# Turning the gathered token rows of a mixture-of-experts feed-forward with VectorE block transposes instead of TensorE transposes

## The reference, cut to what matters

```
gate = xs @ w_gate[e]              # 1024 -> 512
up   = xs @ w_up[e]                # 1024 -> 512
down = (silu(gate) * up) @ w_down[e]   # 512 -> 1024
```

## Time and profile before

| quantity | value |
|---|---|
| median of the three executions | 15,433.22 us |
| span of the profiled execution, first to last instruction | 15,412.0 us |
| time of the median that lies outside that span | 21.2 us |
| PE busy | 14,528.9 us (94%) |
| DVE, ACT, POOL busy | 41%, 21%, 25% |
| mean granted TensorE clock | 0.968 |
| DMA engines' busy share in routed tiles, in shared tiles | about 0.23, 0.62 |

### The profile page before, as it was taken

How to read it: one execution, slowest core, us unless ns; L and a number is a source line. 1 busy time by engine, 2 the same in 40 slices (tenths; PEclk the granted TensorE clock), 3 DMA queues, 4 the chain that set the end, 5 groups by cost and what they waited for, 6 DMA issues and landing times.

```text
span 15412.0 us, 212654 instructions
## 1 busy us (share of the span) xinstructions
PE 14528.9 (94%) x73632; PEld 12344.4 (80%) x73633; DVE 6313.4 (41%) x7679; ACT 3173.3 (21%) x4006; POOL 3896.2 (25%) x3973
## 2 busy tenths in 40 slices
PE   7878877749999999999999999999999999999999
PEld 7777777738888888888888888788888888888888
DVE  8998989941221222212221222322212111444554
ACT  3333333311111112211211222312111111111111
POOL 3344445541111111111111111111111111333333
PEclk9888888869999999999999999999999999999999
DMA  2233332241221222212221222322212111666666
GB/s 69 69 63 66 66 64 63 53 72 60 74 75 59 74 76 105 91 60 73 91 74 58 91 89 91 129 93 102 73 60 75 58 60 42 210 206 204 208 204 204
DMA packets 481191, 1445.61 MB, mean 94 GB/s; under 512 B 94385, under 2 KB 94385, under 8 KB 480834
## 3 DMA queue, kind: packets, MB, share of 16 engines
q0 software_dynamic: 286720, 890.00, 17.3%
q1 hardware_dynamic: 172738, 485.33, 11.5%
q10 hardware_dynamic: 21504, 67.13, 1.1%
HBM read 1037.89 MB, written 421.08 MB: 95 GB/s over the span
## 4 chain that ended last, share of the span: by engine, by line
PE 77%; DVE 0%; DMA 0%; issue 0%; ACT 0%; DVEq 0%; ACTq 0%; SPq 0%; POOLq 0%; POOL 0%
PE gps L1318 24%; PE ups L1318 24%; PE yps L1318 24%; PE xps L1325 4%; PE hps L1358 2%; DVE wlo L1246 0%; DMA raw<-in_L_ffn_w_up_dram 0%; ACT whi L1181 0%; DMA xg<-xnd,idx 0%; DVE yrow L1272 0%; DMA picked<-yd,gidx 0%; ACTq L1063 0%; DVEq L1063 0%; DVE xlo L1246 0%; DVE hlo L1246 0%
## 5 line engine op out<-in xcount | busy, mean ns | idle before, releaser
L1282 DVE TENSOR_TENSOR hb<-hb,ups 128x512 f32<-128x512 f32 x672 | 462.1, 688 | 6196.1 <-ACT hb L1200 6196.1
L1160 POOL DMA_INDIRECT yd<-yrow,yidx x544 | 575.6, 1058 | 7816.9 <-DVE yrow L1296 7816.9
L1318 PE MATMUL gps<-whi,xhi 128*128 128x512 f32 x5376 | 2157.4, 401 | 32.8 <-DVE wlo L1246 29.1
L1318 PE MATMUL ups<-whi,xlo 128*128 128x512 f32 x5376 | 2112.9, 393 | 0.0
L1318 PE MATMUL gps<-wlo,xhi 128*128 128x512 f32 x5376 | 2111.6, 393 | 0.0
L1318 PE MATMUL ups<-whi,xhi 128*128 128x512 f32 x5376 | 2111.3, 393 | 0.0
L1318 PE MATMUL gps<-whi,xlo 128*128 128x512 f32 x5376 | 2110.9, 393 | 0.0
L1318 PE MATMUL ups<-wlo,xhi 128*128 128x512 f32 x5376 | 2094.3, 390 | 0.0
L750 PE MATMUL yps<-khi,thi 128*128 128x288 f32 x4608 | 1481.8, 322 | 337.7 <-ACT ysb L436 193.8
L1200 ACT ACTIVATE hb<-gps 128x512 f32<-128x512 f32 x672 | 402.4, 599 | 6729.3 <-PE ups L1318 6719.1
L1318 PE MATMUL yps<-whi,hhi 128*128 128x512 f32 x5376 | 1725.9, 402 | 4.5 <-DVE hlo L1246 4.5
(11 more groups left out here) (161 smaller groups left out, 20294.0 us busy)
## 6 DMA issues: line engine op xcount, KB each, us to landing
raw<-in_L_ffn_w_gate_dram SPq DMA_DIRECT2D x128, 512.0 KB, 6.0
raw<-in_L_ffn_w_up_dram SPq DMA_DIRECT2D x128, 512.0 KB, 7.6
raw<-in_L_ffn_w_down_dram SPq DMA_DIRECT2D x64, 1024.0 KB, 6.9
cin<-in_ctx_dram SPq DMA_DIRECT2D x64, 512.0 KB, 5.0
xin<-in_x_dram SPq DMA_DIRECT2D x64, 512.0 KB
traw<-kpad SPq DMA_DIRECT2D x64, 512.0 KB, 4.2
xres<-in_x_dram SPq DMA_DIRECT2D x256, 128.0 KB, 2.6
x2d<-xres SPq DMA_DIRECT2D x64, 512.0 KB
```

The costliest lines, as they stand in the source:

```text
L1160: pool.indirect_dma_start(out=yd, in_=yrow[i][:, :], in_offset=None, out_offset=bass.IndirectOffsetOnAxis(ap=yidx[i][:, 0:1], axis=0), bou ...
L1282: dve.tensor_tensor(hb[:, :], hb[:, :], ups[:, :], ALU.mult).then_inc(h_done, 1)
L1318: ins = pe.matmul(ps, rows, w[:, chunk, i * 512:(i + 1) * 512], start=first and n == 0, stop=last_one and n == 2)
```

## The change

The eight PE transposes of the token rows go, with the PSUM tensor `xps`. The gather brings a quarter row per descriptor: four indirect DMAs per tile, where partition 32a+s receives, in slot q, quarter a of the tile's token 4s+q. For this the list is loaded as 32 rows of four numbers and written to four groups of partitions, and POOL adds the quarter's number (`xidx`). One DVE transpose instruction over 128x1024 float32, made of 32x32 blocks (`x_turn`), writes `xt` in SBUF, laid out with token rows along the free dimension. The rows of the gate and up weights are stored in the matching order, outside the kernel, with gate and up side by side, so that one DMA of 1 MB loads two chunks of both; the down weights are stored so that a partition's piece is contiguous. `x_high` and `x_low` read `xt` instead of PSUM.

The orders change too. ACT makes `x_high`(t+1) ahead of silu(t), DVE `x_low`(t+1) ahead of the multiplication, and `x_turn`(t+2) stands in DVE's order behind the split of the gate and up weights and ahead of the sums. POOL makes `load_list` and `gather` ahead of `fetch_picks`. Two of the four `picked` buffers go: pick k uses buffer k % 2, so that picks 2 and 3 can be fetched only when picks 0 and 1 of the same tile have been added. The gated rows keep their PE transposes.

```diff
@@ load_weights(sp, raw, w_ld, gate_up, down, before_unit)
-        for src, c in ((gate, 0), (up, I)):
-            sp.dma_start(raw[:, 2 * q:2 * q + 2, c:c + I],
-                         src[2 * q * P:(2 * q + 2) * P, :].rearrange("(k p) i -> p k i", p=P))\
-                .then_inc(w_ld[q], 16)
+        sp.dma_start(raw[:, 2 * q:2 * q + 2, :], gate_up[:, 2 * q:2 * q + 2, :]).then_inc(w_ld[q], 16)
@@ feed_forward
-        xg = [sb(f"xg{i}", [P, L]) for i in range(2)]
+        xg = [sb(f"xg{i}", [P, QUADS, L // QUADS]) for i in range(2)]
+        xt = sb("xt", [P, KX, P])
-        picked = [sb(f"picked{k}", [P, L]) for k in range(K // 2)]
+        picked = [sb(f"picked{k}", [P, L]) for k in range(2)]
-        xps = es.enter_context(nc.psum_tensor("xps", [P, 1024], F32))
@@ gpsimd
-                pool.dma_start(idx[slot][:, :], lists[bass.ds(row * P, P), :]).then_inc(idx_ld[slot], 16)
+                src = lists[bass.ds(row * P, P), :].rearrange("(o s q) n -> o s (q n)", o=1, q=QUADS)
+                pool.dma_start(idx[slot][:, :], src.to_broadcast([QUADS, SQ, QUADS])).then_inc(idx_ld[slot], 16)
...
-                wait(pool, xT_mm, t - 1 if not isinstance(t, int) else max(t - 1, 0))
+                wait(pool, x_turned, t - 1 if not isinstance(t, int) else max(t - 1, 0))
                 pool.wait_ge(idx_ld[slot], 16 * (turns + 1))
-                settle(pool, pool_turns)
-                pool.indirect_dma_start(out=xg[slot][:, :], out_offset=None, in_=xnd,
-                                        in_offset=bass.IndirectOffsetOnAxis(ap=idx[slot][:, 0:1], axis=0))\
-                    .then_inc(x_ld[slot], 16)
+                pool.tensor_tensor(xidx[slot][:, :], idx[slot][:, :], quad[:, :], ALU.add).then_inc(xidx_ready, 1)
+                pool.wait_ge(xidx_ready, t + 1)
+                for q in range(QUADS):
+                    settle(pool, pool_turns)
+                    pool.indirect_dma_start(out=xg[slot][:, q, :], out_offset=None, in_=quarters,
+                                            in_offset=bass.IndirectOffsetOnAxis(ap=xidx[slot][:, q:q + 1], axis=0))\
+                        .then_inc(x_ld[slot], 16)
...
                 for k in range(K // 2):
-                    if not isinstance(m, int) or m > 0:
-                        pool.wait_ge(pick_used, K // 2 * (m - 1) + k + 1)
+                    if not isinstance(m, int) or m > 0 or k > 1:
+                        pool.wait_ge(pick_used, K // 2 * m + k - 1)
...
             def tile(c):
-                if c.part(-1) is not None:
-                    fetch_picks(c.n(-1 - SH0), c.slot(-1 - SH0), c.part(-1))
                 if c.on(3):
                     load_list(c.n(3), c.slot(3), c.half(3))
                 if c.on(2):
                     gather(c.n(2), c.slot(2), c.half(2))
+                if c.part(-1) is not None:
+                    fetch_picks(c.n(-1 - SH0), c.slot(-1 - SH0), c.part(-1))
@@ scalar
             def x_high(t):
-                act.wait_ge(xT_mm, t + 1)
-                act.activation(xhi[:, :, :].rearrange("p k t -> p (k t)"), xps[:, :], ACT.Copy).then_inc(x_hi, 1)
+                act.wait_ge(x_turned, t + 1)
+                wait(act, gu_mm, t)
+                act.activation(xhi[:, :, :], xt[:, :, :], ACT.Copy).then_inc(x_hi, 1)
...
                 store_sum(c)
+                if c.on(1):
+                    x_high(c.n(1))
                 if c.on():
                     act.wait_ge(gu_mm, t + 1)
@@ vector
+            def x_turn(t, slot, turns):
+
+                dve.wait_ge(x_ld[slot], 16 * QUADS * (turns + 1))
+                wait(dve, x_lo, t)
+                dve.transpose(xt[:, :, :].rearrange("p k t -> p (k t)"),
+                              xg[slot][:, :, :].rearrange("p q (k r) -> p k q r", r=SQ)).then_inc(x_turned, 1)
...
             def tile(c):
                 t = c.n()
+                if c.on(1):
+                    x_low(c.n(1))
                 if c.on():
                     dve.wait_ge(silu_done, t + 1)
                     dve.tensor_tensor(hb[:, :], hb[:, :], ups[:, :], ALU.mult).then_inc(h_done, 1)
                 if c.on(1):
-                    x_low(c.n(1))
...
+                if c.on(2):
+                    x_turn(c.n(2), c.slot(2), c.half(2))
...
+            x_turn(0, 0, 0)
             split_gu(0)
             x_low(0)
+            x_turn(1, 1, 0)
@@ tensor
-            def transpose_rows(t, slot, turns):
-                pe.wait_ge(x_ld[slot], 16 * (turns + 1))
-                for m in range(KX):
-                    last = pe.transpose(xps[:, m * P:(m + 1) * P], xg[slot][:, m * P:(m + 1) * P], ident)
-                last.then_inc(xT_mm, 1)
...
-                if c.on(1):
-                    transpose_rows(c.n(1), c.slot(1), c.half(1))
```

More of the change, by code:

```diff
@@ L204, in expert_weights @@
     one = slice(e, e + 1) if isinstance(e, int) else bass.ds(e, 1)
-    return [A[k][one].rearrange("o a b -> (o a) b") for k in ("w_gate", "w_up", "w_down")]
+    return [A[k][one].rearrange("o p k i -> (o p) k i") for k in ("w_gu", "w_dn")]
 def channel_rows(t, group, quarter):
@@ L948, in _ @@
             f = fields[:, 0:EXPERT_TILES, :]
-            link(dve.tensor_scalar(rows[:, :], f[:, :, F_START], con[:, C_T:C_T + 1], None, ALU.add))
+            link(dve.tensor_scalar(rows[:, :], f[:, :, F_START], con[:, C_POS:C_POS + 1], None, ALU.add))
             link(dve.tensor_tensor(over[:, :], rows[:, :], f[:, :, F_END], ALU.is_ge))
@@ L1052, in feed_forward @@
         acc_ld = [sem(f"acc_ld{i}") for i in range(2)]
-        pick_ld = [sem(f"pick_ld{k}") for k in range(K // 2)]
+        pick_ld = [sem(f"pick_ld{k}") for k in range(2)]
         pool_turns = sem("pool_turns2")
         gidx_ready, yidx_ready = sem("gidx_ready"), sem("yidx_ready")
-        gu_mm, xT_mm, down_mm, hT_mm = sem("gu_mm"), sem("xT_mm"), sem("down_mm"), sem("hT_mm")
+        gu_mm, down_mm = sem("gu_mm"), sem("down_mm")
+        x_turned, hT_mm = sem("x_turned"), sem("hT_mm")
         silu_done, h_done = sem("silu_done"), sem("h_done")
@@ L1069, in _, with before_unit, wait_for @@
         def _(sp):
-            def load(e, weights):
-                def before_unit(q):
+            def before_unit(e):
+                def wait_for(q):
                     if q < GU:
@@ L1076, in before_unit @@
                         sp.wait_ge(lo_dn, DN * (e - 1) + q - GU + 1)
-                load_weights(sp, raw, w_ld, *weights, before_unit)
-            with sp.Fori(1, E) as e:
-                load(e, expert_weights(A, e))
-            for s in range(NE - E):
-                cols = slice(s * I, (s + 1) * I)
-                load(E + s, (A["sw_gate"][:, cols], A["sw_up"][:, cols], A["sw_down"][cols, :]))
+                return wait_for
+            with sp.Fori(1, NE) as e:
+                load_weights(sp, raw, w_ld, *expert_weights(A, e), before_unit(e))
             sp.wait_ge(y_st[0], 16 * SH0 // 2)
@@ L1201, in tile @@
                 if c.on(1):
-                    x_high(c.n(1))
                     if c.part(-1) != 1:
@@ L1305, in tile @@
                         split_dn(entry(dve, t, F_EXPERT, NE - 1))
+            for q in range(QUADS):
+                last = dve.tensor_copy(quad[:, q:q + 1], con[:, C_QUAD:C_QUAD + 1])
+            last.then_inc(quad_ready, 1)
+            x_turn(0, 0, 0)
             split_gu(0)
             x_low(0)
+            x_turn(1, 1, 0)
             walk_tiles(dve, tile)
@@ L1391, in program, with blocks_of_rows, weights @@
         feed_forward(nc, A, keep)
-_INS = ["x", "ctx_2048", "L0_xattn_ssm_kernel", "L0_xattn_D", "L0_ffn_router_w", "L0_ffn_router_bias",
-        "L0_ffn_w_gate", "L0_ffn_w_up", "L0_ffn_w_down", "L0_ffn_sw_gate", "L0_ffn_sw_up", "L0_ffn_sw_down"]
+_INS = ["x", "ctx_2048", "L0_xattn_ssm_kernel", "L0_xattn_D", "L0_ffn_router_w", "L0_ffn_router_bias"]
+def blocks_of_rows(w, chunks):
+    e, _, n = w.shape
+    return w.reshape(e, QUADS, chunks, SQ, n).transpose(0, 1, 3, 2, 4).reshape(e, P, chunks, n)
+def weights(gate, up, down, sw_gate, sw_up, sw_down):
+    import numpy as np
+    parts = [slice(s * I, (s + 1) * I) for s in range(NE - E)]
+    gate = np.concatenate([gate] + [sw_gate[None, :, c] for c in parts])
+    up = np.concatenate([up] + [sw_up[None, :, c] for c in parts])
+    down = np.concatenate([down] + [sw_down[None, c, :] for c in parts])
+    return blocks_of_rows(np.concatenate([gate, up], axis=2), KX), down.reshape(NE, KH, P, L).transpose(0, 2, 1, 3)
 def kernel(**inputs):
@@ L1404 @@
     con, tokens = constants()
+    w_gu, w_dn = weights(*[_np.asarray(inputs["L0_ffn_" + k])
+                           for k in ("w_gate", "w_up", "w_down", "sw_gate", "sw_up", "sw_down")])
     arrays, args = {}, []
-    for name, a in [(n, inputs[n]) for n in _INS] + [("con", con), ("tokens", tokens)]:
+    for name, a in [(n, inputs[n]) for n in _INS] + [("w_gu", w_gu), ("w_dn", w_dn), ("con", con),
+                                                     ("tokens", tokens)]:
```

53 lines of the change are left out of this document (31 added, 22 removed).

## The result

The changed kernel takes 15,459.86 us (median of 20 runs, 15,434.69 to 15,494.29) against 15,430.85 us of the kernel before (20 runs on the same chip): ratio 1.0019, 95% interval 1.0013 to 1.0025. I had forecast 15,019 us. The profiled span is 15,457.1 us where my sum gave 14,998: 459 us are to be explained.

What follows compares the result with a forecast made beforehand. PE, busy 94% of the span, was taken as the bound. Terms -473 (routed), +13 (expert changes), +9 (start), +56 (half 1), -27 (half 0), +8 (tail) sum to -414 us: 15,019 us from 15,433.2, range 14,880 to 15,200.

Steps and rivals of the forecast that it cites:

- A tile without x transposes is 17.82 - 0.87 = 16.95.: Routed tiles: PE saves 0.87 us in each of 544 tiles, other engines staying hidden, -473 us.
- Half 0: First 64 shared tiles: POOL's loop of picks, list, index and four gathers sets 17.4 us per tile, -27 us.
- Half 1: Other 64 shared tiles: a loop through ACT's four stores, x_high, transpose and sum takes 18.65 us, +56 us.
- Rival 2: Shared tiles: slower pick landings and a 2.5 us transpose give 15,370 us, or 15,195 at half; chance of either 0.16.
- Start: Before the first GU: DVE waits for the gather and makes x_turn ahead of the weight split, +9 us.
- the DVE transpose: New 128x1024 transpose on DVE: 1.2 us, between bounds of 0.6 and 2.5.
- routed tiles with every other engine hidden: 544 routed tiles: ACT, DVE and POOL work all fits inside PE's 16.95 us tile.
- changes of expert: At 33 changes of expert GU waits for the first wlo, 0.4 us each, +13 us.
- The tail's +8: Last tile's sum: two buffer exchanges with nothing beside them, about one landing, issue and adds more, +8 us.

Runs made afterwards that it cites:

- the identity's transposes: Changed kernel with three pick buffers and the old PSUM banks, plus eight PE transposes of the constant identity per tile: 15,658.78 us, ratio 1.0145.
- the fast version: Changed kernel with three pick buffers, and xt and the small index tiles allocated behind them so operands stand where they were before: 14,984.84 us, ratio 0.9708.
- with the operands in place: Changed kernel with its two pick buffers, only the operands moved to a position within 256 bytes like that before: 15,314.65 us, ratio 0.9926.
- the fastest one: Changed kernel with three pick buffers, operands where they were before, and the index addition moved between picks 2 and 3: 14,899.67 us, ratio 0.9652.
- tiles of 22.5 us: Changed kernel with three pick buffers, pick 3 fetched behind the quarter gathers and ACT's stores behind silu: 15,761.94 us, ratio 1.0211.

## Why the prediction was wrong

The sign failed. The 459 us of the miss lie in the routed stage (165, of which 150 are the place of the operands), half 0 (213), half 1 (67) and the start (14), as the table of stages has them.

1. *"A tile without x transposes is 17.82 - 0.87 = 16.95."* The 0.87 was right (0.87 for the identity's transposes, and a tile of 16.94 in the fast version). The step assumed that the matmuls keep their pace, and they did not: new tensors ahead of `xg` moved the operands, and each of 72 matmuls lasts (5.60 - 5.50) / 24 = 0.004 us more, some 0.3 us per tile. Measured by itself: 145 us of the time, 149.9 of the routed stage. Without it that stage is 9,324.5 us where my terms gave 9,309. No row of before could show it, and I had no bound for it in the range.
2. *Half 0, "17.4 us".* The loop was the right one, its terms too small. From second add to second add (13511.70 to 13531.91, 20.21 us): to the end of the add 1.28; to pick 3's issue 1.12 (I had 0.5, but pick 2's issue was slow and stands ahead); issue 0.93 (1.1); list 0.76 (0.9); index and wait 1.08 (1.0); four gathers 5.90 (4.8); `gidx` and wait 1.08 (1.0); to pick 1's issue 1.27 (1.4); its landing, up to the add, 6.79 (5.4 with the gap). Nearly all the difference of 2.8 is gathers, pick 2 and landing. The tile shown is a quicker one: the mean of the 63 periods of half 0 is 20.6 us, with 5.4 for the gathers and 6.8 from pick 1's issue to its add. Over the half, then, the landing is the term most in error: with the operands in place, pick 1 lands 6.2 us after its issue on average in half 0, and I had taken 5.2. As for the issues, at the start I had set the one of 2.64 us beside DVE's split against the quick one of 0.98; in this loop, where DVE's adds run beside POOL all the time, I took 0.98 for every issue. Taking out two gathers gave back 300 us.
3. *Half 1, "here I see a new loop".* That loop exists and is the shorter one. Moving the stores away gained nothing, and half 1 goes at 1,245.1 / 63 = 19.8 us per tile, above the 18.65. With half of the gathers the same loop does come last in half 1, at 18.3, so its length was nearly right and naming it the longest was the error. I had summed POOL's loop for half 0 alone, though POOL's order is the same in both halves, and had not put it against the one of 18.65 in half 1. (The product there, 64 x (18.7 - 17.8), is 58 and not 56.)
4. *Rival 2, the exchange costs more*, was the nearest: 22.0 and 19.5 us and 15,370 in full. The mean of its loops is 20.75, near the 20.2 measured, but by halves it is the other way round (20.6 us in half 0 and 19.8 in half 1 were measured), and its time holds nothing for the operands' place, so its nearness is in part luck. I left its far end out of the range, since I had added its parts as mishaps and not seen that slow issues belong to the loop.
5. *Start.* My path from the first issue to GU was 2 us too long. The rest is the end of the first part, which differs between builds: the constants `quad` are written at 3380.75 in the changed kernel and at 3389.54 in the fastest one. POOL's idle time ahead of its first list is 16.78 us, and was 16.77, so the delay lies before it. I have not looked for the cause.
6. *Right:* the DVE transpose (1.238 for 1.2), routed tiles with every other engine hidden, changes of expert. Of the last, PE's waits for `wlo` from 5,000 to 12,500 us rise from 29.1 us in 3 waits to 39.1 in 14, by 10 us, where I had +13 for all.

The tail's +8 was not measured apart.

The change, taken apart: routed stage 444.5 us shorter with the operands in place, of which their new place takes back 149.9; shared stage 317.0 longer; start 22.7 later. That leaves +45 us of span. A third pick buffer, the order of four allocations and the index addition moved by one place give back all but the start.

## What to carry to other kernels

When an engine that was at 25% gets new instructions, close its loop again in every stage, from one buffer's release round to the next, with each issue priced at what it costs beside what the other engine has already begun in that stage, and compare all loops of the stage before naming one. A buffer saved is a wait added: see first what now stands in the queue behind that wait. And when a change adds tensors, compare the pace of untouched instructions before and after; if it differs, move the tensors before looking for anything else.

## What the runs showed of the hardware

- Float32 matmuls with 128x128 stationary and 512 moving columns follow each other at 5.50 / 24 = 0.229 us or at 5.60 / 24 = 0.233, by where `xhi` and its neighbours start within 256 bytes of SBUF. Two builds 128 bytes apart differ by 146 us in 15,000.
- An indirect DMA's issue on GpSimd takes 0.94 us alone. Begun while a DVE instruction with two SBUF inputs is running, it takes up to 2.0 in the shared stage, the surplus being about what that instruction still has to run; begun first, it took 1.02 at most.
- The granted clock fell where PE waited: 0.95 in half 0 of the changed kernel (12,950 to 13,850 us), 0.91 there with tiles of 22.5 us, 1.00 in the fastest version. After a wait of 3.44 us the first eight matmuls of a DN start 0.42 us apart, with a granted clock of 0.53 (13502.30 to 13505.60), and the later ones 0.23, with 0.99. It hardly sets the time here: the final addition that reads this DN starts 11 us after it has ended.
